# A two-pass layer kernel whose second pass stores each strip by itself instead of strips in pairs

## What is computed

```
x = x + conv(group_norm(x))        # group_norm: 8 groups of 2 channels, eps 1e-5
conv(X) = sum over 15 set partitions of {i0, i1, o0, o1} of
          einsum(X reduced, copied or transposed over (i, j), W[k] (16 x 16)) / n^r  + sum(bias)
```

## Time and profile before

| | |
|---|---|
| timed runs, us | 2041.34, 2044.98, 2045.75 (median 2044.98) |
| profiled execution: its own time | 2041.38 us |
| its span | 2039.1 us |
| mean granted TensorE clock | 0.942 |
| TensorE busy (matmul, weight load) | 1630.1 us, 999.9 us |
| VectorE, ScalarE, GpSimd busy | 1333.5, 79.1, 256.5 us |
| HBM read, written | 564.73 MB, 269.09 MB |
| mean of all DMA | 409 GB/s |

### The profile page before, as it was taken

How to read it: one execution, slowest core, us unless ns; L and a number is a source line. 1 busy time by engine, 2 the same in 40 slices (tenths; PEclk the granted TensorE clock), 3 DMA queues, 4 the chain that set the end, 5 groups by cost and what they waited for, 6 DMA issues and landing times.

```text
span 2039.1 us, 43249 instructions
## 1 busy us (share of the span) xinstructions
PE 1630.1 (80%) x19730; PEld 999.9 (49%) x19730; DVE 1333.5 (65%) x1285; ACT 79.1 (4%) x80; POOL 256.5 (13%) x488
## 2 busy tenths in 40 slices
PE   6888888888888858999887778777877777778773
PEld 6877777777777753344333333333333333333331
DVE  5988888888888832677555555555555555555553
ACT  0111111001111100000000000000000000000000
POOL 6333333333333310000000000000000000000000
PEclk9999999999999965999999999999999999999987
DMA  9999999999999980899999999999999999999998
GB/s 376 416 415 414 422 422 423 422 422 422 422 422 422 424 352 0 331 431 431 430 431 431 431 431 431 431 431 431 431 431 430 431 431 430 431 431 431 431 430 372
DMA packets 78957, 834.80 MB, mean 409 GB/s; under 512 B 10617, under 2 KB 10745, under 8 KB 11321
## 3 DMA queue, kind: packets, MB, share of 16 engines
q1 hardware_dynamic: 59208, 564.76, 65.9%
q10 hardware_dynamic: 19696, 269.40, 30.9%
HBM read 564.73 MB, written 269.09 MB: 409 GB/s over the span
## 4 chain that ended last, share of the span: by engine, by line
another core or an unknown queue 47%; DMA 33%; PE 10%; DVE 6%; SPq 2%; issue 1%; POOL 0%; ACT 0%; DVEq 0%; POOLq 0%
DMA early<-pairs 28%; PE ps L763 6%; DVE ring_own L515 5%; DMA out<-early 2%; SPq L317 2%; DMA early<-strip_in 1%; DMA dia_in<-dia 1%; PE ps L742 0%; PE ps L744 0%; PE ps L738 0%; PE ps L698 0%; PE ps L692 0%; PE ps L770 0%; POOL gram_all L365 0%
## 5 line engine op out<-in xcount | busy, mean ns | idle before, releaser
L763 PE MATMUL ps<-ring_own,mixer 128*128 128x512 f32 x1252 | 592.9, 631 | 137.5 <-DMA ring_own<-strip_in 126.8
L668 PE MATMUL ps<-early 128*64 128x66 f32 x17408 | 590.6, 224 | 121.6 <-DMA early<-pairs 114.3
L515 DVE TENSOR_REDUCE ring_own<-early 128x32 f32<-128x2048 f32 x272 | 619.9, 2285 | 84.0 <-DMA early<-pairs 83.6
L668 PEld LDWEIGHTS ps<-early 128*64 128x64 f32 x17408 | 554.6, 138 | 157.4 <-DMA early<-pairs 130.3
L639 DVE SCALAR_TENSOR_TENSOR ring_own<-ps,row_sum,stage 128x512 f32<-128x512 f32 (+3 forms) x233 | 301.6, 1295 | 331.4 <-PE ps L763 331.4
L763 PEld LDWEIGHTS ps<-ring_own,mixer 128*128 128x128 f32 x1252 | 247.0, 202 | 484.6 <-issue 468.9
L763 PE MATMUL ps<-early,mixer 128*128 128x512 f32 x800 | 374.5, 625 | 89.6 <-DMA early<-strip_in 79.0
L639 DVE SCALAR_TENSOR_TENSOR early<-ps,row_sum,stage 128x1024 f32<-128x1024 f32 (+2 forms) x152 | 192.6, 1267 | 197.2 <-PE ps L763 197.2
L763 PEld LDWEIGHTS ps<-early,mixer 128*128 128x128 f32 x800 | 156.2, 200 | 307.5 <-issue 296.1
L365 POOL TENSOR_TENSOR gram_all<-gram_all,stage 128x1024 f32<-128x1024 f32 x68 | 150.5, 2213 | 0.3
L647 DVE SCALAR_TENSOR_TENSOR ring_own<-ps,row_sum,stage 128x488 f32<-128x488 f32 (+43 forms) x308 | 133.4, 475 | 0.0
(11 more groups left out here) (137 smaller groups left out, 133.9 us busy)
## 6 DMA issues: line engine op xcount, KB each, us to landing
early<-pairs SPq DMA_DIRECT2D x272, 1056.0 KB, 18.1
ring_own<-strip_in SPq DMA_DIRECT2D x78, 2048.0 KB, 23.3
out<-ring_own ACTq DMA_DIRECT2D x78, 2048.0 KB, 63.1
early<-strip_in SPq DMA_DIRECT2D x50, 2048.0 KB, 23.3
out<-early ACTq DMA_DIRECT2D x50, 2048.0 KB, 63.4
const<-const_f SPq DMA_DIRECT2D x1, 781.0 KB, 22.2
ring_own<-dia_pair SPq DMA_DIRECT2D x1, 640.0 KB, 21.8
ring_own<-half_in SPq DMA_DIRECT2D x1, 512.0 KB, 36.5
```

The source lines that it names most:

```text
L515: nc.vector.tensor_reduce(part_sum[:, t % sums], vbuf[:, s].rearrange("p (q w) -> p q w", w=FOUR)[:, :, 0:PAIR * SUB].rearrange("p q (c a) ...
L668: last = mm(regions(parity)[lane:lane + WIDE, m // BANK_REGIONS, m % BANK_REGIONS], chunk(slot, k, WIDE), chunk(slot, k, WIDE + MARKS), st ...
L763: last = mm(ps[:, first + at // BANK, 0:piece], mixer[:, :, :].rearrange("p c a -> p (c a)"), buf[:, at:at + piece], start=True, stop=True)
```

## The change

ScalarE's queue now issues a store after every strip. Each moves 128 x 2048 floats, a row of 8 KB for each partition: the left or right half of the unit's 16 KB rows in SBUF and in HBM. A slot's `z_out` is raised twice for each unit, and the waits of the loads count 2 * 16 for each turn. Loads, slots, order and all arithmetic stay.

```diff
                 if turn:
-                    sp.wait_ge(z_out[s], 16 * turn)
+                    sp.wait_ge(z_out[s], 2 * 16 * turn)
                 load(u)
             for s in range(TWOS):
-                sp.wait_ge(z_out[s], 16 * len(range(s, half_strip // 2, TWOS)))
+                sp.wait_ge(z_out[s], 2 * 16 * len(range(s, half_strip // 2, TWOS)))
...
             for p, (u, k, q) in enumerate(order):
-                buf, s, _ = home(u)
-                if k == len(units[u]) - 1:
-                    act.wait_ge(finished, p + 1)
-                    act.dma_start(half_out if s == TWOS else twos_out[units[u][0] // 2], buf).then_inc(z_out[s], 16)
+                _, s, _ = home(u)
+                act.wait_ge(finished, p + 1)
+                act.dma_start(half_out if s == TWOS else twos_out[q // 2][:, k * n:(k + 1) * n],
+                              strip_buf(u, k)).then_inc(z_out[s], 16)
                 if q == half_strip:
```

## The result

The changed kernel is slower: median 2067.14 us of four runs (2066.62 to 2070.39) against 2045.37 us (2041.34 to 2045.89), a ratio of 1.0115 with a 95% interval of 1.0101 to 1.0129, or +21.8 us. The profiled execution of the changed kernel has a span of 2064.4 us, 25.3 more than before. The direction was forecast; the size was 10 us and the range ended at 2062.

What follows compares the result with a forecast made beforehand. It took the DMA engines as the bound, time being bytes over rate. Base 2043.4 us (mean of four times) + 0 start + 0 end + 10 steady gave 2053.4, rounded 2053.5 us; range 2045 to 2062 us.

Steps and rivals of the forecast that it cites:

- Bound by the DMA engines: Both passes: DMA engines are fully busy (share 1.01), so time is bytes over rate once the queues fill.
- nothing at the start: Start of second pass: first store goes out about 3.4 us earlier, which becomes idle time; value 0.
- the gate: Start of second pass: SyncE's queue waits 128.0 us for the diagonal's multiplies at L342, next loads still from 845.76 us.
- The steady term: Steady part of second pass: 124 more store DMAs at a fixed 0.08 us each, about +10 us.
- The end: End of second pass: last store stands behind some 20 us of older stores; value 0, bound -2.45 us.
- No stall on ScalarE's queue: ScalarE's queue after the diagonal: 128 more DMAs issued at 0.34 us each cost nothing.
- Landing times: Second pass: loads land in about 7.4 us instead of 23.3, stores in some 80 us, without changing the sum.
- Rival 1: Steady part: shorter rows cost next to nothing, 0 to 4 us, about 2045.5 us; chance 14%.
- Rival 2: Both ends of second pass: earlier hand-over gains 3.4 us at the start, 2.45 at the end, 2037.5 us; chance 6%.
- Rival 3: Second pass's stores: writing every other 8 KB in HBM lowers the rate to 410 GB/s, 31 us, 2074 us; chance 9%.

Runs made afterwards that it cites:

- e10: The kernel before with each unit's store cut into two DMAs of every other partition, 16 KB rows, issued together: 2046.61 us, ratio 1.0012.
- e1: The kernel before with one store for each unit as before, but every row cut into two of 8 KB: 2046.41 us, ratio 1.0009.
- e2: The changed kernel with the output laid out strip by strip, so each 1 MB store writes without gaps in HBM: 2069.49 us, ratio 1.0136.
- e3: The changed kernel with both strips' stores of a unit issued together after the second strip: 2072.07 us, ratio 1.0147.
- e5: Seven two-strip slots instead of ten, in both kernels: the changed kernel 2081.08 us, the kernel before 2058.14 us.
- e6: The changed kernel with a unit's first store held until the unit three before has landed, at most 6 stores queued: 2063.16 us, ratio 1.0090.
- e11: The changed kernel with every strip's store cut again, four stores of 512 KB with 4 KB rows for each unit: 2074.33 us, ratio 1.0151.
- e7: The changed kernel with the second pass's loads cut too, two DMAs of 1 MB with 8 KB rows for each unit: 2055.89 us, ratio 1.0052.
- e12: The kernel before with each unit's store in two 1 MB DMAs of every other partition, rows cut into two of 8 KB: 2048.30 us, ratio 1.0028.
- e14: The changed kernel with each load cut into two 1 MB DMAs of every other partition, 16 KB rows: 2052.98 us, ratio 1.0038.
- e9: The kernel before with one 4 MB store, rows of 32 KB, for every two units, loads unchanged: 2074.01 us, ratio 1.0139.
- e4: The kernel before with each unit's store cut into two DMAs, lower and upper 64 partitions, 16 KB rows: 2110.58 us, ratio 1.0328.
- e8: The kernel before with only the loads cut in two, 8 KB rows, the stores whole: 2062.72 us, ratio 1.0091.

## Why the prediction was right or wrong

- **Bound by the DMA engines; nothing at the start.** Right. The first store went out at 813.82 us, the gate did not move, and the share stayed at 1.01.
- **The steady term, 124 x 0.08 us = 10 us.** This step failed. It read a fixed price for each DMA of 128 rows from two row sizes, and that price was to stand for all that splitting does. The term measured 16.7 us. What it named costs somewhat less than it took: 128 more DMAs 2.4 us (e10), 992 more rows 2.7 to 6 us (e1), 5 to 8 us together. The larger part, 12 us, are stretched rows, for which the sum had no term. The earlier trace rows hold no trace of them: before has only equal rows and equal DMAs on the two sides. That 10 is not far from 16.7 is thus partly luck; the two numbers don't mean the same thing.
- **The end, 0 us.** The second failed step. I asked only whether the last store stands behind others, which it does, and not whether 16 engines finish together. The earlier trace rows showed 6.7 us of waiting for the last engine already before; it became 15.6 us. Even a steady term of 16.7 with no loss at the end would have come to 2043.4 + 16.7 = 2060 us, just inside the range; the 8.9 us at the end belong to the miss as much as the steady part.
- **No stall on ScalarE's queue.** Wrong, and without a price: issues rose from 0.34 to 5.4 us. The mistake had little weight, since e1 stalls twice as long and loses 2.7 us.
- **Landing times, loads about 7.4 us and stores about 80.** Off: 13.1 and 47.8. The direction for the loads and the turns row by row were right, by the order of the row records. For the stores, the sum did not know that issues stall, so that finished strips wait on ScalarE's side of the queue; no run takes this apart further. That loads beside equal rows land at 13.9 us in e10 as well shows that this time is a weak witness for how queues share.
- **Rival 1 (rows at no cost)** was nearly right about rows (e1) and wrong about the kernel. **Rival 2 (open ends)** is out: the gate did what was said. **Rival 3 (gaps in HBM)** is out by e2; its sign, a full share at a lower rate, did come, from another cause.

Settled: the loss is not the gaps and not the early hand-over; neither the count of DMAs nor the 8 KB rows make more than 3 us of it alone by the times; and the steady part of it doesn't need the full queue. It came in every run that stores each strip by itself beside whole 2 MB loads (the changed kernel, e2, e3, e5, e6, e11). Its stretched rows leave when rows, DMA sizes and walk are all equal (e7); about three quarters of the loss goes when the store goes through whole partitions (e12), and about two thirds when the load DMAs are halved (e14). Open: why the last row but one of a load waits. Unequal rows together with DMAs of unequal size, and the walk over half rows, are both still candidates, and none of them alone explains all runs: e12 has the first and not the second and loses little, e9 has the first and not the second and stretches 4.0%, e14 has unequal rows and the walk and stretches 2.2%. Also open is which engine is late at the end, and why. A wait of over 11 us for it goes with stretched rows and long store landings together; that the one brings the other about is not shown.

## What to carry to other kernels

When a stage is bound by DMA, cut loads and stores alike or not at all: here equal cuts cost only rows, while unequal ones shifted the queues and could stretch rows with the share still at 1. If only the output's layout asks for shorter rows, keep one whole DMA (e1, +2.7 us) rather than two halves side by side (+21.8). Check separately what a split changes: row length and number of DMAs were each nearly free here, which partitions a DMA covers cost 67 us (e4), and the walk was not tested by itself. And price the end by how evenly the engines finish, not only by what is last in the queue.

## What the runs showed of the hardware that I had not expected

- A store DMA over the lower or upper 64 partitions costs much, one over every other partition next to nothing: 2110.58 against 2046.61 us, with store rows of 671 and 612 ns.
- Past some depth of the store queue the issuing engine stalls, in the median 5.4 us an issue in the changed kernel and 10.7 in e1 (at most 11 and 21), and this alone is harmless (e1). By these sums stalls were the rule with 78 to 89 rows and completions queued for each engine, and not with 59 (before, 6.5 x 9), 70 (e10) or 74 (e5 after, 40.7 / 4.94 x 9).
- Loads and stores take turns on an engine row by row while both have rows queued. With unequal rows the queue with the longer ones wins so clearly that the other's DMAs take 49 to 62 us to land (e8, e9) against 23.3 before.
